# Scaling the normalised tokens of six batches on ScalarE instead of VectorE

## The reference

```python
h = tokenise(x)                          # colour maps, relu curves, clip
h = concatenate([h, txt], axis=1)        # (8, 384, 256)
h = h + attn(layernorm(h))               # c_kv = n @ W_DKV; k, v from c_kv; q = n @ W_UQ; causal softmax; @ W_O
h = h + ffn(layernorm(h))                # router softmax, top 2, 8 experts, gelu, bias
# layernorm(x) = (x - mean) / sqrt(var + 1e-5)
```

## Time and profile before

| what | value |
| --- | --- |
| median of 3 runs | 650.83 us (650.32 to 652.74) |
| the profiled execution's own time | 652.22 us |
| its span, first to last instruction | 650.5 us |
| busy over the span | PE 592.4, DVE 412.5, ACT 374.2, POOL 396.7 us |
| shares of the chain that ended last | PE 60%, DVE 8%, ACT 4%, issue 4% |

### The profile page before, as it was taken

One profiled execution on the slowest core, in us unless ns is written; L12 is line 12 of the kernel. 1 busy time (PEld: TensorE's weight loads), 2 busy tenths in 40 slices (PEclk: granted clock), 3 DMA queues, 4 the chain that ended last, 5 costly groups with the idle time before them and its releaser, 6 DMA issues.

```text
span 650.5 us, 13178 instructions
## 1 busy us (share of the span) xinstructions
PE 592.4 (91%) x4776; PEld 490.4 (75%) x4776; DVE 412.5 (63%) x955; ACT 374.2 (58%) x817; POOL 396.7 (61%) x618
## 2 busy tenths in 40 slices
PE   1778899999999999999998999999999999999992
PEld 1454556666666566666574999999999999999992
DVE  5788788889988888687862564444544445343320
ACT  4447787877777776766731645545445454555540
POOL 4503233433655554655847799998898887887223
PEclk9888999999999999998999999999999999999997
DMA  7737666643533232470103645454444444342113
GB/s 235 189 86 188 186 198 181 199 115 84 165 92 107 75 105 82 123 228 31 59 33 107 203 139 114 114 114 114 114 115 115 113 84 88 85 111 46 21 21 37
DMA packets 66705, 75.09 MB, mean 115 GB/s; under 512 B 5944, under 2 KB 61218, under 8 KB 66640
## 3 DMA queue, kind: packets, MB, share of 16 engines
q1 hardware_dynamic: 56352, 60.73, 31.4%
q0 software_dynamic: 9504, 13.00, 11.6%
q10 hardware_dynamic: 784, 0.51, 0.3%
HBM read 31.62 MB, written 22.48 MB: 83 GB/s over the span
## 4 chain that ended last, share of the span: by engine, by line
PE 60%; DVE 8%; ACT 4%; issue 4%; DMA 2%; POOL 2%; SPq 1%; DVEq 0%; ACTq 0%; POOLq 0%
PE t_bank L1877 21%; PE bank L1892 14%; PE s_bank L1892 7%; PE bank L741 4%; DVE mx L1259 3%; PE t_bank L800 2%; PE t_bank L705 2%; PE s_bank L1862 2%; PE bank L835 1%; ACT part L1092 1%; PE t_bank L784 1%; DVE wr L1321 1%; PE bank L753 1%; SPq L417 1%; DMA qs<-mT 1%
## 5 line engine op out<-in xcount | busy, mean ns | idle before, releaser
L1837 DVE TENSOR_TENSOR hl<-h,hh 128x384 fp32r<-128x384 f32 x128 | 110.9, 872 | 146.1 <-ACT h L1800 146.1
L585 POOL TENSOR_SCALAR_AFFINE_SELECT pt<-pt 128x256 f32<-128x256 f32 x192 | 83.4, 443 | 138.1 <-ACT pt L1036 108.2
L1797 ACT ACTIVATE hh<-t_bank 128x384 fp32r<-128x384 f32 x128 | 63.0, 492 | 135.1 <-PE t_bank L1877 132.9
L1259 DVE TENSOR_REDUCE mx<-s_bank 128x2 f32<-128x256 f32 (+2 forms) x192 | 122.3, 682 | 26.2 <-PE s_bank L685 25.4
L1748 POOL DMA_INDIRECT out<-yo,xr x48 | 75.7, 1576 | 56.1 <-ACT yo L1808 45.9
L1735 POOL TENSOR_TENSOR wl<-wr,wh 128x256 fp32r<-128x256 f32 x112 | 95.8, 890 | 1.2
L1036 ACT ACTIVATE pt<-t_bank 128x512 f32<-128x512 f32 x128 | 75.5, 604 | 28.4 <-PE t_bank L705 27.5
L1877 PE MATMUL t_bank<-xh,wh 128*128 128x384 f32 x256 | 87.0, 340 | 1.0 <-DVE xl L1831 1.0
L1877 PE MATMUL t_bank<-xl,wh 128*128 128x384 f32 x256 | 86.5, 338 | 0.0
L1877 PE MATMUL t_bank<-xh,wl 128*128 128x384 f32 x256 | 86.4, 337 | 0.0
L705 PE MATMUL t_bank<-qs,ks 98*128 98x384 bf16 (+2 forms) x384 | 74.8, 277 | 3.1 <-ACT pt L1036 2.2
(11 more groups left out here) (215 smaller groups left out, 1335.7 us busy)
## 6 DMA issues: line engine op xcount, KB each, us to landing
wr<-in_w SPq DMA_DIRECT2D x16, 1024.0 KB, 6.9
qs<-part SPq DMA_DIRECT2D x96, 96.0 KB, 2.2
ks<-part SPq DMA_DIRECT2D x90, 96.0 KB, 2.4
slot_rows<-empty SPq DMA_DIRECT2D x4, 1560.0 KB, 9.2
xr<-slot_rows SPq DMA_DIRECT2D x16, 390.0 KB, 3.3
wr<-in_x SPq DMA_DIRECT2D x7, 768.0 KB, 5.7
out<-hid SPq DMA_DIRECT2D x8, 384.0 KB, 3.2
qs<-mT ACTq DMA_DIRECT2D x62, 3.0 KB
```

The source lines that it names most:

```text
L585: pool.affine_select(out=blocks, in_=blocks, compare_op=ALU.is_ge, fill=0.0, base=0, pattern=[[0, 2], [1, P]], channel_multiplier=-1).then ...
L1259: ins = dve.tensor_reduce(mx[:, p // 2, j, 2 * (p % 2):2 * (p % 2) + 2], pair_region(s_bank, j), AX_X, ALU.max)
L1797: act.activation(hh[:, f, :], h_banks[f % NH], ACT.Gelu_apprx_tanh)
L1837: dve.tensor_tensor(hl[:, f, :], h[f % 2][:, :], hh[:, f, :].bitcast(F32), ALU.subtract).then_inc(hl_done, 1)
```

## The change

Batches 0 and 1 keep the old way. For batches 2 to 7 (`b >= EARLY`, EARLY = 2) the scaling is written as `xn = rstd * hid + lift` with `lift = -mean * rstd`. GpSimd makes `fall = -mean` between its two old instructions, and `lift` behind them; VectorE's `scaled(b + 2)` is taken out of the loop; ScalarE runs one ACTIVATE a tile behind each of the three exponentials of head pair 3, with `rstd` as the per-partition scale and `lift` as the per-partition bias. The first of them waits for `lift` and for the transposes of the batch before.

```diff
+    fall = buf("fall", [P, NT])
+    lift = buf("lift", [P, NT])
...
+    lifted = sem("lifted")
...
             pool.wait_ge(ve_done, b + 1)
+            if b >= EARLY:
+                pool.tensor_scalar(fall[:, :], mv[:, :, 0], -1.0, None, ALU.mult).then_inc(lifted, 1)
             pool.tensor_tensor(rstd[:, :], ve[:, :], neg_half[:, :], ALU.pow).then_inc(rstd_done, 1)
+            if b >= EARLY:
+                pool.wait_ge(rstd_done, b + 1)
+                pool.wait_ge(lifted, 2 * (b - EARLY) + 1)
+                pool.tensor_tensor(lift[:, :], fall[:, :], rstd[:, :], ALU.mult).then_inc(lifted, 1)
...
+        def scaled(b, t):
+            if t == 0:
+                act.wait_ge(lifted, 2 * (b - EARLY) + 2)
+                act.wait_ge(xnT_ps, KC * b)
+            act.activation(xn[:, t, :], hid[:, b, t, :], ACT.Identity, bias=lift[:, t:t + 1],
+                           scale=rstd[:, t:t + 1]).then_inc(xn_done, 1)
...
                 if cur:
                     exps(n, p, 0)
+                if not odd and p == 3 and live(b + 2):
+                    scaled(b + 2, 0)
...
                 if cur:
                     exps(n, p, 1)
+                if not odd and p == 3 and live(b + 2):
+                    scaled(b + 2, 1)
...
                 if cur:
                     exps(n, p, 2)
+                if not odd and p == 3 and live(b + 2):
+                    scaled(b + 2, 2)
...
-                    if p == 3 and live(b + 2):
-                        scaled(b + 2)
                     if p == 3 and live(b - 1) and n < END - 1:
                         residual(b - 1, 0)
```

## The result

The changed kernel takes 662.73 us in the median (661.73 to 665.05, 4 runs) where the kernel before takes 651.79 beside it (650.32 to 653.26). The ratio is 1.0173, with a 95% interval from 1.0149 to 1.0197: 10.9 us slower. The forecast was slower by 5.5 us, 656.3, with a range up to 659.5. The direction is right, the size is half of what happened, and the time lies outside the range.

The account below looks back on a forecast made before the run. No engine alone was the bound; the chain ran through VectorE's three scalings once a batch. Turns summed 1.63 + 0.96 + 2.52 + 0.35 = 5.46, so 650.83 + 5.5 = 656.3 us, range 651.5 to 659.5.

Parts of the forecast that it names:

- Slower, by ScalarE's wait for `lift` in front of its queue: Behind exponential 0, turn 8: ScalarE's first scaling stalls 1.43 us for `lift`; kernel slower by 5.5 us.
- 0.60 us a scaling, 0.49 for the queue: On ScalarE, a 256-column scaling lasts about 0.60 us and delays the queue 0.49 a tile, 1.47 a batch.
- Everything in ScalarE's queue stands behind it: the `query_key` copy ...: ScalarE's queue, turn 8: stall 1.43 plus first tile 0.49 make the `query_key` copy and exponential 1 late by 1.92 us.
- the hole of 1.24 us took up the rest, and +1.08 is left: Before ScalarE's exponential 2, turn 8: the idle hole absorbs part of the delay, leaving exponential 2 late by 1.08 us.
- The heavier rival: TensorE, waiting for exponentials 1 and 2, loses 1.57 us in each of six turns: 9.4 us, 660.2; chance 0.09.
- TensorE's first transposes released by ScalarE's scaling: A batch's first transpose on TensorE: released by ScalarE's last scaling instead of VectorE's residual, starting 0.35 us late.
- The other signs: Profile after: the hole before exponential 2 of p = 3 gone, the period 38.1 us in place of 37.26.
- 0.50 us at most from a lighter VectorE: TensorE's transposes, turn 8: taking 1.14 us from VectorE brings them forward by at most 0.50 us.
- Turn 0, 1.33 to 1.94 us: Turn 0: ScalarE's delay costs 1.33 to 1.94 us, depending on whether DMA issues shrink; 1.63 taken.
- The rule of the Trainium skill that adds and multiplies belong on VectorE: Scaling's price: 0.49 us a tile on ScalarE against 0.38 on VectorE, 2.0 us more engine time over six batches.

Follow-up runs that it names:

- The wait alone: Kernel before plus GpSimd's two new instructions and ScalarE's wait for `lift`, with VectorE still scaling all batches: ratio 1.0099 (1.0066 to 1.0131).
- The work alone: Kernel before plus three spare ScalarE activations of 128 x 256 in the change's places, no new wait, VectorE still scaling: ratio 1.0072 (1.0042 to 1.0102).

## Why the prediction was half right

- *Slower, by ScalarE's wait for `lift` in front of its queue*: right. The forecast had the scaling start 1.43 us behind the copy's old place, with 0.47 for GpSimd's two instructions; measured were 1.50 (1.36 of it idleness) and 0.52. The wait alone makes the kernel slower by 1.0%.
- *0.60 us a scaling, 0.49 for the queue*: right, 0.60 and 0.50. The work alone costs 0.23 us in turns 4 to 8.
- *"Everything in ScalarE's queue stands behind it: the `query_key` copy ..."*: this is the step that failed. The copy was named as delayed, but I never asked who waits for it. +1.92 us was carried only along ScalarE's own stream to exponential 2, where "the hole of 1.24 us took up the rest, and +1.08 is left". But the hole's end was set by TensorE, and TensorE stood in `project`, which waits for that copy's bank. In turn 6, where the changed kernel was 4.21 us behind and the clock was full (its rows stand in the section on the result), `project` is 1.91 us late and exponential 2 behind it 1.99, where the forecast had 1.08. With the third tile ScalarE is 2.48 late, and the hole before exponential 2 of the next turn with what was idle around it gives back 0.73, as forecast: 1.99 + 0.49 - 0.73 = 1.75 a turn, where 1.73 was measured in turn 6, 1.67 in turn 4, and 0.84 was forecast. The sum was short by this one term in turns 4 to 8, and by the same in turn 2: exponential 2 was 1.46 late for a forecast of 0.47, the third tile added 0.49, and two DMA issues that were 0.39 longer did the rest of 2.34. In turn 10, `project` held by 1.70 us cost 1.27 with the clock kept full, where only 0.35 was forecast. Moving one copy ahead of the stall removes it, which shows the cause: turns 2 to 10 fall from 12.03 to 1.60 us (3.4 of the difference is the clock).
- *The clock*: missing in the forecast; the earlier trace rows shows 1.00 in two turns and I took it as given. Behind the new gaps it fell to about half in turns 8 and 10, 3.4 us there. What it adds to the whole kernel is open, as said above. Without these 3.4 us turns 0 to 10 cost 10.5, still nearly twice the 5.46 of the sum, so the clock isn't what made the forecast fail.
- *The heavier rival* came nearest in size, 660.2, with TensorE losing 1.57 us a turn, but had the wrong place: it let TensorE wait for exponentials 1 and 2. Its number is in part luck. It got 0.09.
- *TensorE's first transposes released by ScalarE's scaling*: wrong. They start without idleness in the changed kernel, since TensorE itself is later than the last tile.
- *The other signs*: the hole before exponential 2 was to be gone and was still 0.80 us in turn 6; the period was to be 38.1 us and was 39.0 there (174.05 to 213.06).
- *0.50 us at most from a lighter VectorE*: too low for its own step, since the transposes came 0.65 us earlier with the scalings in the hole; the turns gained 0.24 to 0.26 in 4 to 8 and 0.67 in turn 10, where there are no colour maps on ScalarE.
- *Turn 0, 1.33 to 1.94 us*: right within what turn 0 varies by, 1.90 and 2.01; there is no `project` in that turn.
- *The rule of the Trainium skill that adds and multiplies belong on VectorE* (ScalarE: Activation LUTs, Rules for kernel authors): the trace agrees in the price, 0.50 against 0.38 us a tile, but price isn't what decided. With two of the three activations moved into ScalarE's hole no difference from the kernel before can be told.

## What to carry to other kernels

When work with a new wait is put into an in-order queue, list for every instruction behind it what it frees, PSUM banks too, and not only when it runs; the instruction that cost most here was the one whose bank another engine writes next. A hole in an engine's row belongs to the engine that releases its end: before a delay is set off against it, ask whether the delay reaches that releaser. Put such work where its operand is already there: with the first two of the three scalings a few places later, the cost was too small to measure.

## What the runs showed of the hardware that I had not expected

Gaps of 1.7 us on TensorE, once a batch, left the granted clock at 1.00 behind the gaps of turns 4 and 6 and lowered it to 0.53 to 0.60 over `project` behind those of turns 8 and 10, in two executions of the changed kernel; the eight matmuls that took 1.89 us took 3.1 to 3.65. With 1.5 us of small matmuls in each gap it stayed at 1.00 in turns 2 to 10. The clock fell elsewhere too, in the kernel before as well: to 0.57 from 304.5 to 308.5 us, where TensorE was busy throughout and had last stood idle for 0.48 us. So a fall of the clock in one profile isn't yet an effect of a change; the same stretch in a second profile, and in one with the gap filled, is what one can go by. A 128 x 128 fp32 matmul of this filling shows as two instructions, 0.12 us each.
